# Attention over edges: maximum, subtraction and weighted product joined over two or four quads, and one instruction over four PSUM banks for the edge products of quads 2 and 3

## The reference

```
w_m = (efeat @ W_msg + b_msg).reshape(E, 16, 16)
w_a = (efeat @ W_attn + b_attn).reshape(E, 16, 16)
e1 = w_m * feat[src][:, :, None]
e2 = w_a * feat[src][:, :, None]
seg_max = segment_max(e2, dst)
ex = exp(e2 - seg_max[dst])
attn = ex / segment_sum(ex, dst)[dst]
ft = segment_sum(e1 * attn, dst).sum(axis=1)
```

## Time and profile before

| | |
|---|---|
| time, median of 3 runs | 8973.12 us (8966.02 to 8974.08) |
| span of the profiled execution (first to last instruction) | 8951.1 us |
| the profiled execution's own device time | not given; the median is 22.0 us above the span |
| busy: TensorE, VectorE, ScalarE, GpSimd | 7229.0, 7510.0, 4799.3, 6388.3 us |
| attention stage, steady part | from about 5935 to 8775 us of the span |

### The profile page before, as it was taken

How to read it: one execution, slowest core, us unless ns; L and a number is a source line. 1 busy time by engine, 2 the same in 40 slices (tenths; PEclk the granted TensorE clock), 3 DMA queues, 4 the chain that set the end, 5 groups by cost and what they waited for, 6 DMA issues and landing times. The chain is left out here.

```text
span 8951.1 us, 135582 instructions
## 1 busy us (share of the span) xinstructions
PE 7229.0 (81%) x35152; PEld 4078.3 (46%) x35152; DVE 7510.0 (84%) x11807; ACT 4799.3 (54%) x7730; POOL 6388.3 (71%) x6335
## 2 busy tenths in 40 slices
PE   3888857888888088888888889488888888888884
PEld 3776744555555055555555555233333333333331
DVE  7999956777777388888888888499999999999997
ACT  5999956666666056556666656233333333333333
POOL 6777767777776577777777777376777777677674
PEclk9899967888887589999999999789999999999997
DMA  4222221121111111111111111122222222222223
GB/s 154 65 64 61 64 40 44 45 45 46 46 45 38 20 28 28 33 28 33 28 31 29 29 32 17 20 65 82 75 75 76 75 82 76 75 76 75 81 77 99
DMA packets 499695, 493.19 MB, mean 55 GB/s; under 512 B 181075, under 2 KB 396906, under 8 KB 498731
## 3 DMA queue, kind: packets, MB, share of 16 engines
q1 hardware_dynamic: 299595, 371.60, 12.5%
q0 software_dynamic: 199904, 119.78, 9.7%
HBM read 240.96 MB, written 249.95 MB: 55 GB/s over the span
## 5 line engine op out<-in xcount | busy, mean ns | idle before, releaser
L2525 POOL DMA_INDIRECT attn_got<-tab,attn_line x1760 | 1925.6, 1094 | 778.7 <-issue 504.4
L1983 POOL DMA_INDIRECT sheaf_got<-tab,sheaf_idx x1612 | 1692.1, 1050 | 489.9 <-issue 474.8
L2578 PE MATMUL attn_q<-attn_X,ident 128*128 128x512 f32 x3520 | 1716.2, 626 | 101.1 <-ACT attn_S L2658 92.5
L2072 PE MATMUL sheaf_acc<-sheaf_hot_hi,sheaf_wide 128*128 128x392 bf16 x6696 | 1350.5, 344 | 282.7 <-DVE sheaf_hot_hi L2275 280.9
L1508 POOL DMA_INDIRECT nnconv_got<-tab,nnconv_idx x1116 | 1081.9, 969 | 400.0 <-issue 320.9
L2578 PEld LDWEIGHTS attn_q<-attn_X,ident 128*128 128x128 f32 x3520 | 651.4, 198 | 1190.6 <-issue 1190.6
L2715 DVE TENSOR_TENSOR attn_T<-attn_w,attn_got 128x1024 f32<-128x1024 f32 x880 | 1054.5, 1220 | 150.4 <-PE attn_w L2569 115.2
L2658 ACT COPY attn_S<-attn_q 128x512 f32<-128x512 f32 x440 | 255.9, 582 | 1530.4 <-PE attn_q L2585 1530.4
L1173 POOL DMA_INDIRECT gcn_got<-tab,gcn_idx x868 | 825.9, 952 | 302.3 <-issue 274.7
L2072 PEld LDWEIGHTS sheaf_acc<-sheaf_hot_hi,sheaf_wide 128*128 128x128 bf16 x6696 | 653.6, 106 | 819.1 <-issue 489.7
L1267 PE MATMUL gcn_acc<-gcn_hot,pieces 128*128 128x512 f32 x2604 | 740.2, 442 | 193.9 <-ACT gcn_hot L1321 126.6
(11 more groups left out here) (508 smaller groups left out, 13738.5 us busy)
## 6 DMA issues: line engine op xcount, KB each, us to landing
sums<-attn_S SPq DMA_DIRECT2D x110, 1024.0 KB, 5.2
tops<-attn_S SPq DMA_DIRECT2D x110, 512.0 KB, 3.0
attn_got<-tab,attn_line POOLq DMA_INDIRECT x1760, 2.4
sheaf_got<-tab,sheaf_idx POOLq DMA_INDIRECT x1612, 2.4
gcn_key<-src_key SPq DMA_DIRECT2D x62, 384.0 KB
gcn_blk<-src_blk SPq DMA_DIRECT2D x62, 384.0 KB
nnconv_got<-tab,nnconv_idx POOLq DMA_INDIRECT x1116
nnconv_key<-src_key SPq DMA_DIRECT2D x62, 256.0 KB
```

The costliest lines, as they stand in the source:

```text
L1983: e.indirect_dma_start(out=got[at.b][:, j, D:D + T2], out_offset=None, in_=tab[2], in_offset=indices(idx[at.b], j)).then_inc(s_got[half][a ...
L2072: mm = e.matmul(pacc[k][:, 0:HH], wide[at.b][half][:, part, col, :], hot[:, k * HH:(k + 1) * HH], start=False, stop=False, skip_group_chec ...
L2525: e.indirect_dma_start(out=got[at.b][:, 4 * q + n, :], out_offset=None, in_=tab[3], in_offset=indices(ids[:, q, n, :], D + 2)).then_inc(s_ ...
L2578: e.matmul(to, ident[:, :], X[:, q, :, n, :], start=n == 0, stop=False)
```

## The change

- The maximum's first step is one instruction over four quads instead of two over two quads each.
- `below` is one `tensor_tensor` over two quads, twice a block, instead of a `scalar_tensor_tensor` per quad. The backward chain is `back(2)`, `back(1)`, `below` of quads 2 and 3, `back(0)`, `drop`, `below` of quads 0 and 1.
- `product` is one instruction over two quads, twice a block. `carried` comes before the first instead of behind it.
- `times` of quads 2 and 3 is one instruction over all four banks; quads 0 and 1 keep their halves.
- `attn_w` is one PSUM tensor of four banks. `s_t` counts 6 a block instead of 8 (`TN`, and `TIMES_BY[q]` ahead of quad q), `s_sub` and `s_prod` count 2 instead of 4, and all that wait for them count accordingly.

```diff
-            pw = [ps(f"attn_w{q}", [P, 1024], banks) for q in range(2)]
+            pw_all = ps("attn_w", [P, 2048], banks)
+            pw = [pw_all[:, half * 1024:(half + 1) * 1024] for half in range(2)]
+            TIMES_BY = [sum((2, 2, 1, 1)[:q]) for q in range(QB + 1)]
+            TN = TIMES_BY[QB]
...
-                            turn_wait(e, s_t, at.of(2 * QB, 2 - 3 * QB + QB * half))
+                            turn_wait(e, s_t, at.of(TN, TIMES_BY[(half + 1) * QB // 2] - 2 * TN + 2))
...
-                        turn_wait(e, s_t, at.of(2 * QB, 2 * q + 2))
+                        turn_wait(e, s_t, at.of(TN, TIMES_BY[q] + 2))
...
-                        turn_wait(e, s_prod, at.of(QB, q + 1))
+                        turn_wait(e, s_prod, at.of(2, q // 2 + 1))
...
-                        e.wait_ge(s_sub, at.of(QB, QB))
+                        e.wait_ge(s_sub, at.of(2, 2))
...
+                        if q >= 2:
+                            for n in range(4):
+                                e.wait_ge(s_col[n], at.of(QB, q + 1))
+                            e.tensor_tensor(
+                                T[at.b][:, q, :, :, :].rearrange("p t n (i o) -> p n t i o", o=D),
+                                pw_all.rearrange("p (n t i o) -> p n t i o", n=4, t=2, o=D),
+                                got[at.b][:, 4 * q:4 * q + 4, :].rearrange(
+                                    "p n (t i) -> p n t i", t=2)[:, :, :, :, None].to_broadcast([P, 4, 2, D, D]),
+                                ALU.mult).then_inc(s_t, 1)
+                            return
...
-                        def below(q):
-                            e.scalar_tensor_tensor(
-                                out=Tb[:, q, 0, :, :], in0=Tb[:, q, 0, :, :], scalar=1.0,
-                                in1=ptop[:, q, None, :].to_broadcast([P, 4, CH]), op0=ALU.mult, op1=ALU.subtract).then_inc(s_sub, 1)
-
-                        def product(q):
-
-                            e.wait_ge(s_x, at.of(QB, q + 1))
+                        def below(half):
+                            q = slice(half * QB // 2, (half + 1) * QB // 2)
+                            e.tensor_tensor(Tb[:, q, 0, :, :], Tb[:, q, 0, :, :],
+                                            ptop[:, q, None, :].to_broadcast([P, QB // 2, 4, CH]),
+                                            ALU.subtract).then_inc(s_sub, 1)
+
+                        def product(half):
+
+                            q = slice(half * QB // 2, (half + 1) * QB // 2)
+                            e.wait_ge(s_x, at.of(QB, (half + 1) * QB // 2))
...
-                        for q in range(0, QB, 2):
-                            n = ch.do(larger(two[:, q:q + 2, :, :].rearrange("p q n c -> p q (n c)"),
-                                             Tb[:, q:q + 2, 0, 0:2, :].rearrange("p q n c -> p q (n c)"),
-                                             Tb[:, q:q + 2, 0, 2:4, :].rearrange("p q n c -> p q (n c)")))
+                        n = ch.do(larger(two[:, :, :, :].rearrange("p q n c -> p q (n c)"),
+                                         Tb[:, :, 0, 0:2, :].rearrange("p q n c -> p q (n c)"),
+                                         Tb[:, :, 0, 2:4, :].rearrange("p q n c -> p q (n c)")))
...
-                        for q in range(QB - 2, -1, -1):
-                            n = back(q)
-                            below(q + 1)
-                            ch.wait(n)
+                        n = back(2)
+                        ch.wait(n)
+                        n = back(1)
+                        below(1)
+                        ch.wait(n)
+                        ch.wait(back(0))
                         e.scalar_tensor_tensor(out=drop[:, :], in0=So[:, QB - 1, 0:CH], scalar=1.0, in1=ptop[:, 0, :],
                                                op0=ALU.mult, op1=ALU.subtract).then_inc(s_top, 1)
                         below(0)
                         if more:
                             times(nxt, 2)
-                        product(0)
                         e.wait_ge(s_scale, at.of(1, 1))
...
                                                op0=ALU.mult, op1=ALU.mult).then_inc(s_carried, 1)
-                        product(1)
+                        product(0)
                         if more:
                             times(nxt, 3)
-                        product(2)
-                        product(3)
+                        product(1)
```

More of the change, by code:

```diff
@@ L2708, in times @@
                         if q == 0 and at.k >= 2 and 0 in halves:
-                            e.wait_ge(s_prod, at.of(QB, -QB))
+                            e.wait_ge(s_prod, at.of(2, -2))
                         if q % 2 == 0 and 0 in halves:
                             e.wait_ge(s_got[q // 2][at.b], at.half(16 * EH, 16 * EH))
+                        if q >= 2:
[8 more added lines that the diff above has]
+                            return
                         for half in halves:
@@ L2759, in a_block @@
                             times(nxt, 0, (0,))
-                        e.wait_ge(s_t, at.of(2 * QB, 2 * QB + 2))
-                        for q in range(0, QB, 2):
-                            n = ch.do(larger(two[:, q:q + 2, :, :].rearrange("p q n c -> p q (n c)"),
-                                             Tb[:, q:q + 2, 0, 0:2, :].rearrange("p q n c -> p q (n c)"),
-                                             Tb[:, q:q + 2, 0, 2:4, :].rearrange("p q n c -> p q (n c)")))
+                        e.wait_ge(s_t, at.of(TN, TN + 2))
+                        n = ch.do(larger(two[:, :, :, :].rearrange("p q n c -> p q (n c)"),
+                                         Tb[:, :, 0, 0:2, :].rearrange("p q n c -> p q (n c)"),
+                                         Tb[:, :, 0, 2:4, :].rearrange("p q n c -> p q (n c)")))
                         if more:
@@ L2812, in _ @@
                         times(At(0), q)
-                    walk(e, NBQ, a_block, ch, 3 + QB + QB - 1, head=4)
+                    walk(e, NBQ, a_block, ch, 2 + QB + QB - 1, head=4)
                     e.wait_ge(s_state, NBQ * QB + 2)
```

## The result

The changed kernel takes 9331.49 us (median of 4 runs, 9322.91 to 9337.0); the kernel before, on the same occasion, 8970.73. The ratio is 1.0407, 95% interval 1.0393 to 1.0422: slower by 361 us. I had forecast 9114 us in a range to 9185. The direction and the place were right. The forecast loss was too small by a factor of 2.6.

What follows compares the result with a forecast made beforehand. The prediction took a loop through VectorE and TensorE as the bound. A turn of 27.65 plus 1.0 for the clock, against 27.31, is +1.34 us over about 105 blocks: +141 us, 9114 us, range 9010 to 9185.

Steps and rivals of the forecast that it cites:

- R: The prediction's zero point in a block: the start of the first half of times(nxt, 1) on VectorE.
- the joined passes: VectorE: a 2048-element pass lasts 2.29 us and spaces the next by 2.20 instead of 2.26, four PSUM banks included.
- times(nxt, 2) at 9.99: VectorE, behind the backward chain: starts 9.99 us after R instead of 9.84, two opened waits costing more than two joins save.
- product(0) at 12.79: VectorE, behind carried: joined product of quads 0 and 1 runs 12.79 to 15.08; quad 0's alone ran 12.11 to 13.33.
- matrices(nxt, 3) behind an idle 2.07: TensorE: the idle gap ahead of matrices(nxt, 3) grows from 1.98 to about 2.07 us.
- quad_sum(at, 0) at 15.47: TensorE: starts 0.39 us after the joined product's end, behind a new idle gap of 1.90 us.
- matrices(at+2, 0) at 18.10: TensorE: starts 2.63 us after quad_sum(at, 0), at 18.10 instead of 17.48; the next R follows 9.55 us later.
- the clock's term: TensorE: one low-clock dip of 3.42 us a block, beginning at 14.1, with 2.05 us counting half: +1.0 us a turn.
- bound of two dips: TensorE: if each of the two idle gaps draws its own dip, the clock costs up to 2.3 us a turn.
- Rival 1: TensorE's new gap draws no more dips, or they end before quad_sum(at, 0): 9009 to 9046 us; chance 0.17.
- Rivals 2 and 3: VectorE: 2, joins return the whole fixed cost, 8969 us, chance 0.06; 3, tensor_tensor at 16-bit pace, about 8730 us, 0.05.
- Rival 4: Both TensorE gaps draw a dip, or ScalarE's second exponential delays product(0): turn over 29.3, above 9185 us; chance 0.08.

Runs made afterwards that it cites:

- the run with only the first gap filled: The changed kernel plus two unread float32 TensorE products a block, only in the idle gap ahead of matrices(nxt, 3): 9081.58 us, ratio 1.0136.
- the split product: The changed kernel with quad 0's product its own instruction again ahead of carried, quad 1's behind it, other joins kept: 8996.29 us, ratio 1.0039.
- the late signal alone: The kernel before, nothing joined, with only the signal for quad 0's product given together with that of quad 1: 9336.15 us, ratio 1.0415.

## Why the prediction was wrong

By its own steps, in us after R, forecast and measured in the block above:

- the joined passes: 2.29, measured 2.28; spacing 2.20, measured 2.20 (7019.10 to 7021.30, 7021.30 to 7023.50). Right, four banks included.
- times(nxt, 2) at 9.99: 10.00. product(0) at 12.79: 12.80. matrices(nxt, 3) behind an idle 2.07: 2.07. quad_sum(at, 0) at 15.47, behind an idle 1.90: 15.50 and 1.93. All right, and the waits moved as I said.
- matrices(at+2, 0) at 18.10 plus the clock's term of 1.0: 20.89. From there to the next R 9.55 plus nothing: 9.91. **The clock's term is the step that failed.** What the turn is at full clock can be read in the run with only the first gap filled, in its 66 turns without a low stretch: 27.84, in the same steps 15.50, then 2.74 to matrices(0) and 9.59 to the next R, where I had 15.47, 2.63 and 9.55. So 0.19 of the miss is my working without a dip, and the clock's term is 30.72 - 27.84 = 2.9 and not 1.0. I had taken one dip of 3.42 us a block, beginning in the middle between the two gaps, so that 2.05 of it count half. The runs show one stretch of 6.8 us that begins less than 1 us ahead of the sum's start, so that some 6 us of it lie on the loop and count half: the six matmuls take 5.39 instead of 2.74, and 0.3 more comes behind. The prediction's bound of two dips, "up to 2.3", falls short too, by 0.6; it stands there without its working.
- the sum: 3.41 more a turn than 27.31, times 105, is 358 us; measured 361. From the parts, 27.84 and half of the 6 us give 30.8 a turn, 370 us.

Rival 1 (the clock behaves) is refuted by the clock column. Rivals 2 and 3 are refuted by the spacing of 2.20. Rival 4 is what came, by its first half; the second exponential was in time. I had given it 0.08. The reason for that low chance was that I argued from the mean of possible positions of a dip; but in the changed kernel it begins at nearly the same place of every block.

The kernels that still have dips point the same way. The mean turn is 27.31 in the kernel before, in the split product, with the maximum and times joined, and with the subtraction joined, though their turns without a dip range from 26.9 to 27.2. Where such a turn is shorter, more blocks have a dip: 85 of 98 at 26.91, 63 of 97 at 27.05, 29 of 97 at 27.20. (The split product, at 27.04, has 50 of 98, with longer turns where they come.) So small edits on the loop showed neither as a gain nor as a loss. A later signal cost more than itself: 0.6 us of it 1.70 us a turn, 1.7 us of it 3.41, with the full change and with the late signal alone. With one of the two gaps filled the mean took values between, 28.24 and 28.34. What sets the mean is not tested; that filling the gaps removes the dips and leaves the plain turn (27.07, 26.94, 27.83) is shown.

## What to carry to other kernels

When a join moves a completion signal later, price the signal for its receiver first: here seven instructions fewer were worth at most 0.4 us a block by the spacing of 2.20 against 2.26, and one signal 1.7 us later cost 3.4. If the receiver is TensorE, look where it idles and what lies right behind: a second gap near an old one can put the low clock on the critical sum, and a few unread products in the gap bring the clock back. Join VectorE passes that read PSUM rather than passes over SBUF alone when GpSimd issues gathers beside them.

## What I had not expected of the hardware

- The low clock lasted 6.8 us in one piece when two idle stretches (2.07 and 1.93 us) stood 1.14 us apart, and 3.4 us, in two blocks of three, when one of 1.99 stood alone. An idle 0.84 in the place of the 1.93 still drew stretches that slowed the sum to 5.46 or 4.51 us.
- Four kernels whose turns without a dip were 26.9 to 27.2 us had the same mean turn of 27.31 us.
- A gather's issue on GpSimd grew from 0.94 us to 2.67 on average when it began under a joined product of 2.28 us, with both inputs in SBUF, and not under a pass that reads PSUM.
